# A conditioned feed-forward block in two layers on one core: scaling, adds and masking moved to GpSimd, the residual of slot 0 and the router's low rows moved forward

## The reference

```python
y = einsum('bet,bt->be', x, arange(T) < length) / length
g = x * sigmoid(conv5(y))[:, :, None]                     # gated x, per row
ffn = bitlinear(silu(bitlinear(g, w_gate)) * bitlinear(g, w_up), w_down)
x = x + ffn                                               # 512 -> 1376 -> 512
delta = lora_B @ lora_A * 0.5                             # 512 x 512
wq = codebook[searchsorted(thresholds, (W + delta) / scale)] * scale
z = x @ (wq + delta).T
x = x + z @ W_base.T + b_base + experts(z)                # softmax over 4 experts
```

## Time and profile before

| | us |
|---|---|
| median of 3 runs | 153.93 (153.88 to 154.12) |
| the profiled execution | 153.92 |
| its span, first to last instruction | 152.1 |
| mean granted clock of TensorE | 0.989 |
| chain that ended last | PE 50%, DVE 27%, ACT 10%, issue 8%, DMA 2% of the span |
| ScalarE's copy of a transposed hidden row (L639, L640), one | 0.31 and 1.26 |
| ScalarE's rounding of a hidden row (L631), one | 1.44 |

### The profile page before, as it was taken

One profiled execution on the slowest core, in us unless ns is written; L12 is line 12 of the kernel. 1 busy time (PEld: TensorE's weight loads), 2 busy tenths in 40 slices (PEclk: granted clock), 3 DMA queues, 4 the chain that ended last, 5 costly groups with the idle time before them and its releaser, 6 DMA issues.

```text
span 152.1 us, 2134 instructions
## 1 busy us (share of the span) xinstructions
PE 138.4 (91%) x661; PEld 84.7 (56%) x661; DVE 114.1 (75%) x302; ACT 96.1 (63%) x156; POOL 11.0 (7%) x31
## 2 busy tenths in 40 slices
PE   6779999998799967898579999999999999999993
PEld 2256665753356544446234545454576766797792
DVE  2799999989999999999978856998996031035561
ACT  3799998996997975965365659797663403400200
POOL 7000000000000033200004200000000000000000
PEclk9999999999999999999968999999999999999999
DMA  5999999849600430603100905150400000000193
GB/s 172 336 402 421 419 414 404 323 130 396 225 0 0 86 45 5 129 0 69 26 0 0 166 2 107 22 97 2 95 0 4 0 0 0 4 0 0 63 377 112
DMA packets 19486, 19.22 MB, mean 126 GB/s; under 512 B 13474, under 2 KB 13858, under 8 KB 19476
## 3 DMA queue, kind: packets, MB, share of 16 engines
q1 hardware_dynamic: 19476, 19.10, 39.8%
HBM read 13.82 MB, written 2.10 MB: 105 GB/s over the span
## 4 chain that ended last, share of the span: by engine, by line
PE 50%; DVE 27%; ACT 10%; issue 8%; DMA 2%; SPq 0%; ACTq 0%; DVEq 0%
PE bank L971 15%; PE bank L918 12%; ACT tern_d L526 6%; PE bank L881 6%; PE bank L887 6%; DVE hmax L1322 5%; DVE raw_gate L1319 4%; PE bank L929 3%; DVE junk L1158 2%; DMA cond<-in_cond_w 2%; DVE rmax L1208 2%; ACT cond L492 2%; PE bank L978 1%; DVE tern_i L1203 1%; PE bank L863 1%
## 5 line engine op out<-in xcount | busy, mean ns | idle before, releaser
L881 PE MATMUL bank<-tern_g,head_sb 128*128 128x464 bf16 (+1 forms) x96 | 22.6, 357 | 1.0 <-DVE tern_u L1204 0.8
L887 PE MATMUL bank<-tern_u,head_sb 128*128 128x464 bf16 (+1 forms) x96 | 22.5, 357 | 0.6 <-DVE raw_gate L1319 0.6
L918 PE MATMUL bank<-tern_d,delta 128*128 128x512 bf16 (+1 forms) x88 | 22.0, 399 | 0.5 <-DVE tern_d L1204 0.5
L971 PE MATMUL bank<-m_h,fr 128*128 128x512 f32 (+1 forms) x72 | 22.3, 378 | 0.0
L1319 DVE TENSOR_TENSOR raw_gate<-bank,wbt 128x464 f32<-128x464 f32 (+1 forms) x24 | 15.1, 631 | 4.2 <-ACT wbt L624 3.7
L624 ACT ACTIVATE wbt<-bank,s_g 128x464 f32<-128x464 f32 (+1 forms) x24 | 14.9, 633 | 3.4 <-PE bank L881 3.3
L1322 DVE TENSOR_REDUCE hmax<-raw_gate 128x1 f32<-128x464 f32 (+1 forms) x24 | 15.1, 631 | 0.8
L631 ACT ACTIVATE raw_gate<-raw_gate,hq 128x1376 int16<-128x1376 f32 x8 | 11.5, 1438 | 6.5 <-DVE hq L1329 6.5
L918 PEld LDWEIGHTS bank<-tern_d,delta 128*128 128x128 bf16 (+1 forms) x88 | 9.0, 103 | 11.5 <-issue 1.9
L887 PEld LDWEIGHTS bank<-tern_u,head_sb 128*128 128x128 bf16 x96 | 9.3, 98 | 10.0 <-DVE raw_gate L1319 1.2
L796 PE MATMUL bank<-wbt,cond 128*128 128x512 f32 x32 | 14.8, 599 | 0.0
(11 more groups left out here) (177 smaller groups left out, 226.8 us busy)
## 6 DMA issues: line engine op xcount, KB each, us to landing
raw_gate<-in_w_gate_t SPq DMA_DIRECT2D x4, 688.0 KB, 7.4
raw_up<-in_w_up_t SPq DMA_DIRECT2D x4, 688.0 KB, 12.3
xs<-in_x SPq DMA_DIRECT2D x8, 256.0 KB, 13.2
out_x<-xs SPq DMA_DIRECT2D x7, 256.0 KB, 2.2
raw_down<-in_w_down_t SPq DMA_DIRECT2D x2, 768.0 KB, 5.4
cond<-in_cond_w SPq DMA_DIRECT2D x4, 256.0 KB, 4.6
wbt<-in_w_base_t SPq DMA_DIRECT2D x4, 256.0 KB, 9.2
raw_down<-in_w_down_t SPq DMA_DIRECT2D x2, 512.0 KB, 7.6
```

The source lines that it names most:

```text
L881: mm = pe.matmul(bank_g[n % 2][:, 0:w], xq_t[:, b % 2, k, :], tern_g[:, k, f0:f0 + w], start=(k == 0), stop=(k == KH - 1))
L887: mm = pe.matmul(bank_u[n % 2][:, 0:w], xq_t[:, b % 2, k, :], tern_u[:, k, f0:f0 + w], start=(k == 0), stop=(k == KH - 1))
L918: mm = pe.matmul(bank_down[:], h_t[0:rows, b % 2, j, :], tern_d[0:rows, j, :], start=(j == 0), stop=(j == KF - 1))
L971: pe.matmul(bank_y[n_res][:, h0:h1], a[:, b, k, :], m[:, k, h0:h1], start=(n == 0), stop=False)
```

## The change

- GpSimd scales blocks 1 to 3 of `cond`, one instruction of 512 columns each with the scale spread over it, in place of ScalarE's twelve. ScalarE keeps block 0, and each of its four pieces counts on a semaphore of its own, for which VectorE's first normalise waits piece by piece.
- GpSimd adds the deltas (`w_eff`) in place of VectorE. Its eight small instructions that build row masks now stand between the second and the third of them.
- After the last codebook product GpSimd compares the columns with the length and multiplies by x for slots 5 to 7, into mask slots that are free by then; ScalarE sums the products (`masked_sum`, in iteration 2 behind `rounded_down(3)`) in place of VectorE's x_sum(5) to x_sum(7).
- The maxima of the first two chunks of a hidden row are written right behind the row, so that the maximum over the third chunk takes them in and L1326 goes. The tiles behind the row move by 8 elements.
- VectorE's order: residual(0) and the router's low rows come before hidden_chunk(3, 1); x_max of slots 5 and 6 comes at the end of iteration 2, of slot 7 after y_safe(2).

```diff
--- before.py
+++ after.py
@@ -167,10 +167,11 @@
 
         with nc.sbuf_tensor("masks", [P, SLOTS, H], F32R) as mask_sb:
             pass
-        with nc.sbuf_tensor("raw_down", [P, KF, H], F32) as raw_down:
+        with nc.sbuf_tensor("raw_down", [P, SLOTS, H], F32) as raw_down:
             pass
         fr = sb("fr", [P, 4, KH * H], F32R)
         mask = [mask_sb[:, i, :] for i in range(SLOTS)]
+        masked = raw_down[:, KF + 1:KF + 1 + NB - GROUPS[2][0], :]
         x1t_h = fr[:, 0:2, :].rearrange("p a (b k e) -> p (a b) k e", b=4, k=KH)
         x1t_l = fr[:, 2:4, :].rearrange("p a (b k e) -> p (a b) k e", b=4, k=KH)
 
@@ -223,13 +224,13 @@
         wbt_flat = wbt[:].rearrange("p k c -> p (k c)")
         silu = wbt_flat[:, 0:2 * CHUNKS[0][1]].rearrange("p (i f) -> p i f", i=2)
 
-        hbuf = [raw[0][:, i * F:(i + 1) * F] for i in range(2)]
-        patterns = raw[0][:, 2 * F:4 * F].bitcast(I16)
+        hrow = [raw[0][:, i * (F + NC - 1):(i + 1) * (F + NC - 1)] for i in range(2)]
+        hbuf = [row[:, 0:F] for row in hrow]
+        patterns = raw[0][:, 2 * F + 8:4 * F].bitcast(I16)
         h_i = patterns[:, 0:2 * KF * P].rearrange("p (i f) -> p i f", i=2)
-        h_bits = raw[0][:, 2 * F:4 * F].bitcast(BF16)[:, 0:2 * KF * P].rearrange("p (i f) -> p i f", i=2)
+        h_bits = raw[0][:, 2 * F + 8:4 * F].bitcast(BF16)[:, 0:2 * KF * P].rearrange("p (i f) -> p i f", i=2)
         ht_i = patterns[:, 2 * KF * P:3 * KF * P].rearrange("p (j e) -> p j e", j=KF)
         xt_i = patterns[:, 3 * KF * P:3 * KF * P + 2 * H].rearrange("p (i k e) -> p i k e", i=2, k=KH)
-        hmax = sb("hmax", [P, 2, NC])
         hred = sb("hred", [P, NB])
         harow = sb("harow", [P, NB])
         hrec = sb("hrec", [P, NB])
@@ -274,6 +275,7 @@
         ident_done = sem("ident_done")
         eps_done = sem("eps_done")
         delta_ps = sem("delta_ps")
+        condn0_done = sem("condn0_done")
         condn_done = sem("condn_done")
         norm_done = sem("norm_done")
         inv_done = sem("inv_done")
@@ -295,6 +297,10 @@
         value_done = sem("value_done")
         weff_done = sem("weff_done")
         qx_done = sem("qx_done")
+        len_done = sem("len_done")
+        below_done = sem("below_done")
+        masked_done = sem("masked_done")
+        xsum_done = sem("xsum_done")
         ymean_done = sem("ymean_done")
         conv_ps = sem("conv_ps")
         ycond_done = sem("ycond_done")
@@ -440,6 +446,31 @@
             pool.iota(part[:], [[0, 1]], 0, 1, allow_small_or_imprecise_dtypes=True).then_inc(iota_done, 1)
             pool.iota(t_iota[:], [[1, H]], 0, 0, allow_small_or_imprecise_dtypes=True).then_inc(iota_done, 1)
             pool.memset(ones[:], 1.0).then_inc(iota_done, 1)
+
+            def scaled_weight(k):
+                pool.wait_ge(inv_done, 1)
+                pool.wait_ge(ld_cond[k], 16)
+                v = cond[:, k, :].rearrange("p (g i) -> p g i", g=KH)
+                pool.tensor_tensor(v, v, scl_inv[:, k, :].unsqueeze(2).broadcast_to([P, KH, GROUP]),
+                                   ALU.mult).then_inc(condn_done, 1)
+
+            def w_eff(k):
+                pool.wait_ge(delta_done, min(k + 2, KH))
+                pool.wait_ge(value_done, k + 1)
+                pool.tensor_tensor(cond[:, k, :], cond[:, k, :], delta[:, k, :], ALU.add).then_inc(weff_done, 1)
+
+            def masked_x(b):
+                m = masked[:, b - GROUPS[2][0], :]
+                pool.wait_ge(ld_x[b], 16)
+                pool.wait_ge(len_done, 1)
+                pool.tensor_scalar(m, t_iota[:], len_f[:, b:b + 1], None, ALU.is_lt).then_inc(below_done, 1)
+                pool.wait_ge(below_done, b - GROUPS[2][0] + 1)
+                pool.tensor_tensor(m, m, xs[:, b, :], ALU.mult).then_inc(masked_done, 1)
+
+            for k in range(1, KH):
+                scaled_weight(k)
+            w_eff(0)
+            w_eff(1)
             pool.wait_ge(iota_done, 3)
             pool.tensor_scalar(low_row[:], part[:], float(2 * ZC), None, ALU.is_ge).then_inc(rows_done, 1)
             pool.tensor_scalar(tmp_row[:], part[:], float(3 * ZC), None, ALU.is_equal).then_inc(rows_done, 1)
@@ -454,6 +485,11 @@
             pool.tensor_scalar(fold_tmp[:], diff[:, 0:ZL], float(ZL), None, ALU.is_equal).then_inc(rows_done, 1)
             pool.wait_ge(rows_done, 7)
             pool.tensor_tensor(fold_two[:], fold_two[:], fold_tmp[:], ALU.add).then_inc(rows_done, 1)
+            w_eff(2)
+            w_eff(3)
+            pool.wait_ge(cb_ps, KH)
+            for b in range(GROUPS[2][0], NB):
+                masked_x(b)
 
             def x_quantise(b):
                 pool.wait_ge(qx_done, 2 if b < GROUPS[2][0] else 3)
@@ -484,15 +520,12 @@
             act.activation(scl_inv[:], slog, ACT.Exp, scale=-1.0).then_inc(inv_done, 1)
             act.activation(scl[:], slog, ACT.Exp).then_inc(scl_done, 1)
 
-            def scaled_weight(k):
-                act.wait_ge(inv_done, 1)
-                act.wait_ge(ld_cond[k], 16)
-                for g in range(KH):
-                    c = slice(g * GROUP, (g + 1) * GROUP)
-                    ins = act.activation(cond[:, k, c], cond[:, k, c], ACT.Copy, scale=scl_inv[:, k, g:g + 1])
-                ins.then_inc(condn_done, 1)
-
-            scaled_weight(0)
+            act.wait_ge(inv_done, 1)
+            act.wait_ge(ld_cond[0], 16)
+            for g in range(KH):
+                c = slice(g * GROUP, (g + 1) * GROUP)
+                act.activation(cond[:, 0, c], cond[:, 0, c], ACT.Copy,
+                               scale=scl_inv[:, 0, g:g + 1]).then_inc(condn0_done, 1)
 
             def diagonals(i):
 
@@ -507,10 +540,8 @@
 
             act.wait_ge(ident_done, 2)
             act.wait_ge(step_done, 1)
-            for n, i in enumerate(T_ORDER):
+            for i in T_ORDER:
                 diagonals(i)
-                if n == 3:
-                    scaled_weight(1)
             act.wait_ge(scl_done, 1)
 
             def weight_sum(i, k, src, rows=P):
@@ -529,10 +560,8 @@
                 act.wait_ge(ld_gate[k], 16)
                 weight_sum(0, k, raw_gate[:, k, :])
                 if k == 0:
-                    scaled_weight(2)
                     delta_out(3)
                     delta_out(0)
-                    scaled_weight(3)
                     delta_out(1)
                 if k == 1:
                     delta_out(2)
@@ -566,6 +595,12 @@
                 if b >= 2:
                     act.wait_ge(gu_ps, NC * (b - 1))
                 act.activation(xq_t[:, b % 2, :, :], src, ACT.Copy).then_inc(xt_done, 1)
+
+            def masked_sum(b):
+                i = b - GROUPS[2][0]
+                act.wait_ge(masked_done, i + 1)
+                act.activation(masked[:, i, :], masked[:, i, :], ACT.Copy,
+                               accum_out=ysum[:, b:b + 1]).then_inc(xsum_done, 1)
 
             def conv_out(g):
                 b0, b1 = GROUPS[g]
@@ -690,6 +725,8 @@
                     x_evacuate(1)
                 if b == 2:
                     rounded_down(3)
+                    for i in range(GROUPS[2][0], NB):
+                        masked_sum(i)
                 if b == 3:
                     gate_silu(2)
                 if b < NB and b != 1:
@@ -1097,13 +1134,16 @@
 
             def normalise(k):
 
-                dve.wait_ge(condn_done, k + 1)
+                if k > 0:
+                    dve.wait_ge(condn_done, k)
                 if k < KH - 1:
                     dve.wait_ge(delta_ps, k + 1)
                 else:
                     dve.wait_ge(delta_done, 1)
                 for g in range(KH):
                     c = slice(g * GROUP, (g + 1) * GROUP)
+                    if k == 0:
+                        dve.wait_ge(condn0_done, g + 1)
                     src, inv = (bank_delta[k][:, c], inv_part) if k < KH - 1 else (delta[:, k, c], scl_inv)
                     ins = dve.scalar_tensor_tensor(cond[:, k, c], src, inv[:, k, g:g + 1], cond[:, k, c],
                                                    ALU.mult, ALU.add)
@@ -1129,16 +1169,12 @@
                                          scl[:, k, :].unsqueeze(2).broadcast_to([P, KH, GROUP]),
                                          ALU.add, ALU.mult).then_inc(value_done, 1)
 
-            def w_eff(k):
-                dve.wait_ge(delta_done, min(k + 2, KH))
-                dve.wait_ge(value_done, k + 1)
-                dve.tensor_tensor(cond[:, k, :], cond[:, k, :], delta[:, k, :], ALU.add).then_inc(weff_done, 1)
-
             def lengths():
                 dve.tensor_copy(act_f[:], act_i)
                 link(dve.tensor_copy(len_f[:], len_i))
                 dve.tensor_scalar(act_n[:], act_f[:], 0.0, float(NE), ALU.is_lt, ALU.mult)
-                link(dve.reciprocal(len_r[:], len_f[:]))
+                dve.reciprocal(len_r[:], len_f[:]).then_inc(len_done, 1)
+                dve.wait_ge(len_done, 1)
 
             def selectors():
```

(26 more changed lines are left out.)

## The result

| | before | after |
|---|---|---|
| median of 4 runs each, us | 153.91 (153.83 to 154.12) | 159.14 (158.46 to 159.90) |
| ratio, 95% interval | | 1.034 [1.029, 1.039] |
| the profiled execution, us | 153.92 | 158.46 |
| its span, us | 152.1 | 156.6 |
| mean granted clock | 0.989 | 0.967 |

The change costs 5.2 us. I had forecast 152.2, with a range to 156.4: wrong in its sign, and the result lies beyond the range. The likeliest rival, at 157.0, was nearer.

A forecast was written before the change was run, and what follows sets the result against it. VectorE was taken to bound from 31 to 76.5 us, TensorE from 84.80 to 140.00, with a stall between. 153.9 less a 4.0 us lead plus 2.3 for GpSimd meetings gave 152.2; own range 150.5 to 153.5, whole range 149.6 to 156.4.

The forecast's parts named there:

- the price of GpSimd: Cost of GpSimd's new instructions to VectorE: six uncovered meetings at 0.38 us each, 2.3 us in all.
- The price of one meeting: 0.38 us lost by VectorE, from one meeting at 59.66 us of GpSimd's quantising with VectorE's rounding.
- The number of meetings: Six uncovered: one at the first masks, one at masks(2), four between 32 and 40 us.
- The cost of GpSimd's own instructions: Thirteen large new instructions: 1.24 us as upper end, 0.77 as lower; comparisons 0.55 in the blocked case.
- The blocked rival: GpSimd stops VectorE's short SBUF steps until it ends, mainly 31 to 40 us: 7.1 us lost, 157.0; chance 0.37.
- The undisturbed lead: Gain over the whole kernel if GpSimd disturbs nothing: 4.0 us, giving 149.9.
- the maxima: L1326 disappears, 0.19 us a slot in VectorE's queue; four slots before the joint: 0.76 us gained.
- VectorE's wait for the high rows: Before x1_transposes(0), L1373 waits for ScalarE's high rows; about 0.75 us of VectorE's time goes there.
- the late silu(2, 2): ScalarE's three new sums delay silu(2, 2), ending at 64.9 where VectorE wants it at 64.15: 0.8 us lost.
- the loss by the transpose of h(3): In the DMA queue it stands behind x(5)'s transpose; silu(5, 0) comes late for gate_up(5, 2): 1.2 us lost.
- the three sums: x_sum(5) to x_sum(7) leave VectorE, 68.94 to 71.32 us: 2.4 us saved, 0.8 lost to a later silu.
- the join: Hand-over from VectorE to TensorE, 71.43 to 77.91 us; TensorE's 2.62 us idle and slow clock there both go.

The follow-up runs named there:

- experiment 6: The changed kernel without its GpSimd adds and masked sums; GpSimd scales blocks 1 to 3, but starts only when two masks are done: 153.93 us, ratio 1.001.
- experiment 9: The changed kernel with only the masked sums on GpSimd, begun after the second hidden product, two before x_quantise(2), one behind; ScalarE sums before rounded_down(3): 151.01 us.

## Why the prediction was wrong

*The step that failed* is the price of GpSimd: "At 0.38 each, the only price that the trace has, six cost 2.3 us." Taking the parts out shows a cost of 7.1 us, and that is what is left after all that the parts gained. It failed in three ways.

- The price of one meeting. The 0.38 us came from a meeting with GpSimd's quantising, which has one input of 512 elements. For such neighbours it holds: beside the comparisons VectorE lost 0.37 to 0.43 us each time. But ten of the thirteen new instructions have two inputs, and no meeting with one of those was in the trace. There it is not a surcharge but a wait until GpSimd's instruction ends: 0.85, 0.75, 0.97 and 0.89 us on steps of 0.15 to 0.23 that began just after it, 0.54 to 1.06 in all eight. Whether the number of inputs or the operation makes the difference, no run separates.
- The number of meetings. I counted six; the profiled execution has eleven, which lengthen VectorE's instructions by 8.3 us. "VectorE's masks follow each other without gaps in which GpSimd could enter" is refuted by experiment 6: three scalings put 2.36 us between six such masks. The changed kernel shows it too: the mask at 21.29, the second of seven in a row, took 1.50 us for 0.48 beside an add.
- The cost of GpSimd's own instructions. I had the comparison at 0.55 to 0.77 us, by the quantising. It takes 1.57 alone and 1.91 in the mean beside VectorE. The adds and products were well placed: 1.24 estimated, 1.27 measured undisturbed, 1.1 for the scaling with its spread operand.

The blocked rival gave these costs 7.1 us. That this is the measured difference is partly luck: the measured one already has the parts' gains in it, and the items differ (comparisons at 0.55 where VectorE lost 0.4, 2.6 us before 31 us where it lost 3.2, and no clock). It came out at 157.0 instead of 159.1 because it shares the lead of 4.0 us with the other cases.

*The undisturbed lead* of 4.0 us, the base of all my cases, was not reached by any version. Where the meetings are avoided, the kernel is 1.9 us faster without the GpSimd parts and 2.9 with the sums of x(5..7) in place. The remaining 1.1 would have to come from the adds, the scalings and the earlier start that they give; none of them was seen without its meetings, so it stays open. Its single steps: the maxima 0.8 (I said 0.76); VectorE's wait for the high rows 0.91 (0.75); the late silu(2, 2) 0.83 (0.8); the loss by the transpose of h(3) 0.66 of TensorE's waiting (1.2, and that by a slip: 5.2 us before the landing at 89.1 is 83.9 and not 85.4, which leaves no loss and a lead of 5.2); the three sums 1.0 net (1.6, as 2.4 less 0.8). A VectorE that comes sooner waits longer for ScalarE's high rows, 1.45 us in experiment 9 where I had 0.75. The stall moves to that wait, and the sums' gain is cut by it.

*The clock.* I had the drop behind an idle TensorE in the account of the join, and it went as forecast. I did not ask whether the change opens such gaps elsewhere. It does, at 10.45 us (2.16 idle) and 41.57 us (2.35 idle): both stretches have a granted clock of 0.92 instead of 1.00.

*What would show it*, as I had listed: x transposes later than 37.4 us (41.57) and ternaries longer by half (the three of the up weight take 0.99 in the mean, for 0.64) both spoke for the blocked case, while the masks' mean rose only from 0.48 to 0.54; x1_transposes(0) did not begin before 77 us, since the 7.0 us lost by 48.87 outweigh what the join won. ScalarE waited 2.14 us for the transpose of h(3), about as before, so that term was not where the time went.

The weighing of the evidence is the error behind the sum: a price from one meeting was used for instructions of another kind, and the rival that fitted that meeting was held back because there were so few. The kernel before had few because GpSimd did almost nothing in it.

## What to carry to other kernels

Before work goes to an idle GpSimd, look at what VectorE does at that moment. If it works with a PSUM operand or reduces, the work is nearly free (experiment 9); if it is a string of short dependent steps in SBUF, a GpSimd instruction with two inputs costs what is left of its duration, however small the step that meets it, and a comparison or an iota some 0.4 us where they meet. And place the moved work in GpSimd's and ScalarE's queues by who waits behind it: the same three sums gave nothing at one place of the queues and 1.0 us at another.
